# An adjacency GNN pair on one core: fewer matmuls in P, diagonals on GpSimd, setup and last group in a new order

## What is computed

```python
h = relu(layernorm(x))
z_l, z_g, v = h @ W_lang.T, h @ W_grav.T, h @ W_V.T
A_l = relu(cosine(z_l, z_l)) * not_eye          # rows of z_l normalized
A_g = exp(-|z_g_n - z_g_m|**2 / (2 sigma**2)) * not_eye
K   = w_l * rows(A_l * adj) + (1 - w_l) * rows(A_g * adj)   # rows(): divided by the row's sum
x = x + (K @ v) @ W_O.T
h = relu(layernorm(x))
x = x + (adj * adj).T @ h + bias                # per batch
```

## Time and profile before

| | |
|---|---|
| median of 3 runs | 1214.26 us |
| profiled execution | 1213.74 us, span 1212.0 us |
| TensorE busy | 1190.9 us, 98% of the span, 5968 matmuls |
| VectorE busy | 1120.8 us, 92%, 1919 instructions |
| ScalarE busy | 707.0 us, 58% |
| GpSimd busy | 609.5 us, 50%, 988 instructions |
| chain that ended last | TensorE 94%, VectorE 3%, ScalarE, DMA, issue and SPq 1% each |
| chain by line | L1040 50%, L1131 27%, L1109 15% |

### The profile page before, as it was taken

The page is one execution under the profiler, slowest core; times in us unless marked ns, Lnnn a source line. Parts: engine busy times, 40 slices in busy tenths (PEclk is TensorE's granted clock), DMA queues, the critical chain, the costliest instruction groups (busy, mean ns, idle before and its releaser), DMA issues.

```text
span 1212.0 us, 22868 instructions
## 1 busy us (share of the span) xinstructions
PE 1190.9 (98%) x5968; PEld 1009.5 (83%) x5968; DVE 1120.8 (92%) x1919; ACT 707.0 (58%) x1326; POOL 609.5 (50%) x988
## 2 busy tenths in 40 slices
PE   7999999999999999999999999999999999999996
PEld 6887888888888888888888888888888888888884
DVE  6678999999999999999999999999999999999878
ACT  5355556666556666555656555666655566655544
POOL 2103655545565555565454566554556545546543
PEclk9999999999999999999999999999999999999998
DMA  7333555554554564555565455555455556445412
GB/s 258 100 120 90 166 161 166 190 176 154 170 168 149 178 193 154 165 165 157 168 194 170 150 175 163 157 181 188 152 170 165 151 169 199 159 158 159 136 48 104
DMA packets 182416, 193.85 MB, mean 160 GB/s; under 512 B 20352, under 2 KB 131584, under 8 KB 182400
## 3 DMA queue, kind: packets, MB, share of 16 engines
q1 hardware_dynamic: 181824, 193.33, 51.2%
q10 hardware_dynamic: 576, 0.33, 0.1%
HBM read 103.09 MB, written 90.50 MB: 160 GB/s over the span
## 4 chain that ended last, share of the span: by engine, by line
PE 94%; DVE 3%; ACT 1%; DMA 1%; issue 1%; SPq 1%; POOL 0%; ACTq 0%; DVEq 0%
PE ring L1040 50%; PE ring L1131 27%; PE p_ps L1109 15%; PE ring L1158 1%; DVE x_ring L750 0%; DMA x_ring<-in_L_gnn_W_lang 0%; SPq L256 0%; DVE chain L900 0%; ACT h L481 0%; PE ring L1167 0%; DMA h<-p_dram 0%; DVE deg L716 0%; SPq L286 0%; DVE K L730 0%; DVE hT_lo L669 0%
## 5 line engine op out<-in xcount | busy, mean ns | idle before, releaser
L398 POOL TENSOR_TENSOR h_lo<-h2f,h_hi 128x512 fp32r<-128x512 f32 x124 | 157.1, 1298 | 301.7 <-ACT h_hi L584 301.6
L1040 PE MATMUL ring<-hT_hi,Lw_hi 128*128 128x512 f32 x640 | 249.4, 390 | 4.2 <-DVE hT_lo L689 1.5
L1040 PE MATMUL ring<-hT_hi,Lw_lo 128*128 128x512 f32 x640 | 249.0, 389 | 0.0
L1040 PE MATMUL ring<-hT_lo,Lw_hi 128*128 128x512 f32 x640 | 249.0, 389 | 0.0
L502 ACT ACTIVATE y_hi<-ring 128x512 fp32r<-128x512 f32 x256 | 148.5, 592 | 111.8 <-PE ring L1040 109.0
L552 ACT ACTIVATE v_hi<-ring 128x512 fp32r<-128x512 f32 x128 | 76.4, 598 | 227.5 <-PE ring L1131 158.8
L1131 PE MATMUL ring<-MT_hi,hT_hi 128*128 128x512 f32 x512 | 203.0, 397 | 0.3 <-DVE v_lo L669 0.3
L1131 PE MATMUL ring<-MT_lo,hT_hi 128*128 128x512 f32 x512 | 199.9, 390 | 0.0
L1131 PE MATMUL ring<-MT_hi,hT_lo 128*128 128x512 f32 x512 | 199.5, 390 | 0.0
L383 POOL TENSOR_TENSOR x_ring<-x_ring,bias_sb 128x512 f32 (+1 forms) x120 | 166.2, 1406 | 48.1 <-DVE KT_lo L746 48.1
L669 DVE TENSOR_TENSOR y_lo<-ring,y_hi 128x512 fp32r<-128x512 f32 x256 | 166.9, 681 | 19.6 <-ACT y_hi L502 19.6
(11 more groups left out here) (187 smaller groups left out, 2503.1 us busy)
## 6 DMA issues: line engine op xcount, KB each, us to landing
x_ring<-in_x SPq DMA_DIRECT2D x32, 1024.0 KB, 5.3
out<-x_ring SPq DMA_DIRECT2D x128, 256.0 KB, 2.5
h_dram<-h SPq DMA_DIRECT2D x62, 512.0 KB, 3.4
h_turned<-h_dram SPq DMA_DIRECT2D x248, 128.0 KB, 3.3
p_dram<-chain SPq DMA_DIRECT2D x62, 256.0 KB, 2.1
h<-p_dram SPq DMA_DIRECT2D x248, 64.0 KB, 2.6
rn_cols<-rn_dram SPq DMA_DIRECT2D x31, 256.0 KB, 3.9
k_dram<-chain SPq DMA_DIRECT2D x31, 256.0 KB, 2.0
```

The costliest lines, as they stand in the source:

```text
L398: pool.tensor_tensor(h2[1][:, b], h2f[:, b], h2[0][:, b].bitcast(F32), ALU.subtract)\
L1040: mm = pe.matmul(out, lhsT, rhs, start=(k == 0), stop=(k == len(terms) - 1))
```

## The change

- P: in the first row block (a = 0) the third pass, hT_lo·y_hi, is dropped: 8 matmuls for 4 batches and not 12. So that S still has it, y of that block takes its pass hT_lo with M0, the diagonal block that isn't halved, and not with Lw_hi; ScalarE makes two M0 copies in setup.
- `diagonal` of all groups but the last goes to GpSimd. GpSimd's order is now: wait for `k_ready`, two `add_bias`, four `h2_lo`, wait for `kt_split`, both diagonals, `row_norms`. VectorE: `kt_lo`, `squares(0)`, `v_lo(0)`, `squares(1)`, the clip.
- Setup: x(0) is loaded ahead of W_grav, which comes in four loads, and x(1) waits for the last of them; x_stats(0) stands ahead of W_grav's split; TensorE starts with 20 transposes of the identity, and transposes h(0) in the middle of W_grav's product; Lw of l = 1 is finished behind h; all of W_O is transposed inside iteration 0; group 1 is normalized after all y blocks of iteration 0.
- Last group: `shift` after v_hi(0), one of the four adds and the statistics behind the row factors, KT_hi ahead of v_hi(3), two layer 1 products ahead of K·v, the factors of group 30 in two halves, and GpSimd's h2_lo and last factors interleaved otherwise.

The core of the diff ("..." for lines left out; moves of adj_sb and adj2 into the tile chain, and bookkeeping of banks and semaphores, are left out too):

```diff
@@ -228,6 +231,17 @@
         spread = y_rows[0][:, 1, 0:P]
+        select = diag_of[:, :, :].rearrange("p l m -> p (l m)").unsqueeze(1).to_broadcast([P, GB // 2, 2 * P])
+        def diagonal(eng, g, q):
+            half = slice(q * GB // 2, (q + 1) * GB // 2)
+            if q == 0:
+                wait_for(eng, k_stored, 16 * g)
+            eng.wait_ge(p_copied, 2 * g + q + 1)
+            eng.tensor_tensor(diag[:, half].rearrange("p b l m -> p b (l m)"),
+                              P_sb[:, half].rearrange("p b l m -> p b (l m)"), select, ALU.mult)\
+               .then_inc(diag_ready, 1)
@@ -307,11 +321,14 @@
                 sp.dma_start(raw_l[:, c], w_rows[:, c]).then_inc(w_loaded[f"l{c}"], 16)
-            sp.dma_start(raw_g, w_grav.rearrange("(c p) n -> p c n", p=P)).then_inc(w_loaded["g"], 16)
             load_x(0)
+            g_rows = w_grav.rearrange("(c p) n -> p c n", p=P)
+            for c in range(C):
+                sp.dma_start(raw_g[:, c], g_rows[:, c]).then_inc(w_loaded[f"g{c}"], 16)
...
             sp.wait_ge(x_loaded, 16)
+            sp.wait_ge(w_loaded[f"g{C - 1}"], 16)
@@ -355,23 +372,24 @@
                                    base=0, pattern=[[-1, P]], channel_multiplier=1).then_inc(ident_ready, 1)
-            def std_factors(g, bn, bn_done, t, step):
-                pool.wait_ge(bn_done, GB * (g + 1))
+            def std_factors(g, bn, bn_done, t, step, b0=0, b1=GB, steps=0):
+                bn, t = bn[:, b0:b1], t[:, :, b0:b1]
+                pool.wait_ge(bn_done, GB * g + b1)
@@ -407,12 +425,18 @@
                 if lag:
+                    pool.wait_ge(k_ready, i)
+                    add_bias(i - 2, 0)
+                    add_bias(i - 2, 1)
...
                         h2_lo(i - 2, b)
-                    pool.wait_ge(kt_split, i)
-                    add_bias(i - 2, 0)
-                    add_bias(i - 2, 1)
+                if after:
+                    if before:
+                        pool.wait_ge(kt_split, i)
+                    for q in range(2):
+                        diagonal(pool, i, q)
@@ -425,7 +449,9 @@
                         .then_inc(bias_split, 1)
-                    norm2(i - 1)
+                    pool.wait_ge(h2_done, GB * (i - 1))
+                    for q in range(2):
+                        std_factors(i - 1, bn2, bn2_done, ln2, ln2_step, q * HALF, (q + 1) * HALF, LN_STEPS * q)
@@ -451,18 +477,18 @@
                     .then_inc(ln2_rstd, 1)
+            h2_lo(g - 1, 0)
             last_factors(0)
-            h2_lo(g - 1, 0)
             h2_lo(g - 1, 1)
+            h2_lo(g - 1, 2)
             last_factors(1)
-            h2_lo(g - 1, 2)
@@ -502,20 +528,23 @@
                         n += 1
-                        if not before and n <= 2:
-                            factor_hi(C + 2 * n - 2)
-                            factor_hi(C + 2 * n - 1)
+                        if not before:
+                            for q in {2: [C], 3: [C + 1], 4: [C + 2, C + 3], 5: [0, 1], 6: [2], 7: [3]}.get(n, []):
+                                factor_hi(q)
...
                             exponentials(i - 1)
-                        if after and n == 5:
+                        if before and after and n == 5:
...
                             w_g_K_g(i - 1)
-                        if after and n == 7:
+                        if before and after and n == 7:
                             normalize(i + 1, GB // 2)
+                if not before:
+                    normalize(i + 1, 0)
+                    normalize(i + 1, GB // 2)
@@ -544,6 +572,8 @@
                         exponentials(i)
+                    if not after and b == GB - 1:
+                        kt_copy(i)
@@ -554,10 +584,9 @@
                         w_g_K_g(i)
-                    if b == 1 and after:
+                    if b == (1 if after else 0):
...
                 if not after:
-                    kt_copy(i)
@@ -565,6 +594,8 @@
                     act.wait_ge(ln2_rstd, 2 * (1 + b // (GB // 2)))
+                elif isinstance(g, int) and g == NG - 2:
+                    act.wait_ge(ln2_step, LN_STEPS * (g + 1 + b // HALF))
@@ -624,6 +657,8 @@
                     act.wait_ge(setup_mm, C * l + c + 1)
+                    if c == 0:
+                        act.activation(M0[:, l], banks[c][:, 0:P], ACT.Copy)
@@ -801,8 +832,10 @@
                         if not before:
-                            for q in {1: [C], 2: [C + 1], 3: [C + 2, C + 3], 4: [0, 1], 5: [2], 6: [3]}.get(n, []):
+                            for q in {2: [C], 3: [C + 1], 4: [C + 2, C + 3], 5: [0, 1], 6: [2], 7: [3]}.get(n, []):
                                 factor_lo(q)
+                            if n == 3:
+                                x_stats(1, 0, GB)
@@ -813,9 +846,12 @@
                             turn_K(i - 1)
-                        if after and n == 6:
+                        if before and after and n == 6:
...
                             turn_blocks(i + 1, 1)
+                if not before:
+                    turn_blocks(i + 1, 0)
+                    turn_blocks(i + 1, 1)
@@ -830,12 +866,10 @@
                 if before:
-                    diagonal(i, 0)
...
                     squares(i, 0)
-                    diagonal(i, 1)
+                    v_lo(0)
                     squares(i, 1)
-                    v_lo(0)
@@ -888,21 +922,11 @@
                 dve.tensor_tensor(A, p_ps[:, :, :, :], P_sb, ALU.add).then_inc(s_ready, 2)
-            select = diag_of[:, :, :].rearrange("p l m -> p (l m)").unsqueeze(1).to_broadcast([P, GB // 2, 2 * P])
-            def diagonal(g, q):
+            def squares(g, q):
...
                     wait_for(dve, p_shifted, g)
-                    wait_for(dve, k_stored, 16 * g)
-                dve.wait_ge(p_copied, 2 * g + q + 1)
-                dve.tensor_tensor(diag[:, half].rearrange("p b l m -> p b (l m)"),
-                                  P_sb[:, half].rearrange("p b l m -> p b (l m)"), select, ALU.mult)\
-                   .then_inc(diag_ready, 1)
-            def squares(g, q):
-                half = slice(q * GB // 2, (q + 1) * GB // 2)
@@ -920,28 +943,30 @@
                     lo(v[1][:, b], bank(n + v_use(b, True)), v[0][:, b], hi + b + 1).then_inc(drained, 1)
-                diagonal(i, 0)
+                diagonal(dve, i, 0)
...
                 squares(i, 0)
-                diagonal(i, 1)
+                diagonal(dve, i, 1)
...
                 v_lo(0)
-                for b in range(GB):
+                for b in range(3):
                     add(i - 1, b, n + 1 + b)
-                dve.wait_ge(drained, use + G_USES + 1 + GB)
-                dve.wait_ge(ln2_step, LN_STEPS * (i - 1))
-                stats(i - 1, 0)
...
                 row_factors(i)
+                add(i - 1, 3, n + 1 + 3)
+                dve.wait_ge(drained, use + G_USES + 1 + 3)
+                dve.wait_ge(ln2_step, LN_STEPS * (i - 1))
+                stats(i - 1, 0)
+                combine(i)
+                stats(i - 1, 1)
                 v_lo(1)
-                combine(i)
+                kt_lo(i)
                 v_lo(2)
-                stats(i - 1, 1)
-                kt_lo(i)
                 v_lo(3)
+                dve.wait_ge(drained, use + G_USES + 1 + GB)
@@ -1043,9 +1066,13 @@
                 free(use)
-                product(bank(n), [t for c in range(a + 1) for t in passes(
+                terms = [t for c in range(a + 1) for t in passes(
                     [w[:, l, blk[a, c]] for w in Lw],
-                    [w[:, c].rearrange("p b m -> p (b m)") for w in hT])]).then_inc(g_done, 1)
+                    [w[:, c].rearrange("p b m -> p (b m)") for w in hT])]
+                if a == 0:
+                    terms[1] = (M0[:, l], terms[1][1])
+                product(bank(n), terms).then_inc(g_done, 1)
@@ -1090,11 +1117,13 @@
                     for l in range(2):
+                        if not before and l == 1:
+                            pe.wait_ge(side_split, a + 1)
...
                         n += 1
-                        if not before and n == 2:
-                            transposes_w_o(C // 2)
-                            transposes_w_o(C // 2 + 1)
+                        if not before and 2 <= n <= 3:
+                            transposes_w_o(2 * n - 4)
+                            transposes_w_o(2 * n - 3)
@@ -1104,6 +1133,7 @@
                         terms = passes([w[:, a, b] for w in hT], [w[:, a, b].rearrange("p l m -> p (l m)") for w in y])
+                        terms = terms[:2] if a == 0 else terms
@@ -1151,6 +1181,10 @@
                 return passes([w[:, e, c * P:(c + 1) * P] for w in parts], [w[:, e, c * P:D] for w in parts])
+            pe.wait_ge(ident_ready, 1)
+            for _ in range(WARM):
+                pe.transpose(bank(C - 1)[:, 0:P], ident[:, :], ident[:, :])
@@ -1160,6 +1194,10 @@
             for c in range(C):
+                if c == C // 2:
```

(20 more changed lines are left out.)

60 lines of the change are left out of this document (28 added, 32 removed).

## The result

The changed kernel takes 1218.71 us (median of 8 runs, 1216.85 to 1219.85), the kernel before 1214.35 us on the same chip (8 runs): ratio 1.0034, 95% interval 1.0024 to 1.0044. It is slower by 0.3%, where 1197.5 us, 1.4% faster, was forecast. The profiled execution has a span of 1217.4 us against 1212.0.

The account below looks back on a forecast made before the run. TensorE bounds the kernel at 35.88 us a group; afterwards the loop through all queues does, at 35.59. From 1213.7 us, P(31) ending 11.9 earlier and the last group's 4.3 leave 1197.5 us, range 1189.5 to 1209.

Parts of the forecast that it names:

- Rival A: Group loop: TensorE stays the bound, at a period of 35.4 us with no gaps; 1191.8 us, chance 0.20.
- rival C: GpSimd's diagonals: each costs 1.57 us and not 1.27, the loop becomes 36.2 us; 1214 us, chance 0.07.
- The place of TensorE's wait: Group loop: TensorE's K·v or V(1) held by KT_lo or v_lo, some 0.2 us a group.
- The loop after the change: From one first add to the next through rn_cols and K: five terms sum to 35.59 us, 35.76 before.
- the term from k_ready to the first add: KT_lo 8.3, two diagonals 2.54, squares 1 0.69, clip 0.16 less 0.1, hand-overs 0.15: 11.74 us, before 11.91.
- GpSimd's queue, plus 0.55: KT_lo can't finish before GpSimd's six operations end, k_ready + 7.7, plus about 0.55: 8.3 us.
- the issue of rn_cols: Loop term from the end of turn_p(1) to the issue of rn_cols: 2.31 us.
- the three other terms: First add to the end of turn_p(1) 8.29 us, rn_cols' landing 3.9, landing to k_ready 9.35.
- the 1.06 us of diagonal 0: VectorE's diagonal before the change, set against GpSimd's 1.27; the trace was said not to show a factor of 2.
- Rival D: K's return: K lands 7.6 us after k_ready, not 6.9, KT_lo ends at 9.0, loop 36.3; 1217 us, chance 0.10.
- Setup and first groups: y(0) at 24.4 us, net 2.4 earlier, bounds 1 and 4; first add of iteration 1 2.8 earlier.
- The last group: After P(31): reordered chain gains 4.3 us, bounds 2 (GpSimd's factors, unhidden) and 6 (none of these delays).

Follow-up runs that it names:

- e4: Changed kernel with P's two turned halves made earlier on VectorE and ScalarE's shift of P moved earlier: 1209.92 us, ratio 0.9958 to the kernel before.
- e9: Changed kernel with diagonal 0 ahead of KT_lo, diagonal 1 behind it, then h2_lo(2) and (3); squares(1) and clip ahead of v_lo(0): 1197.39 us, ratio 0.9862.
- e12: Changed kernel with the setup of the kernel before (W_grav ahead of x(0), no 20 first transposes): 1216.79 us, ratio 1.0028 to the kernel before.
- e3: Changed kernel with the diagonals back on VectorE and GpSimd's and VectorE's orders as before: 1207.93 us, ratio 0.9942 to the kernel before.

## Why the prediction was wrong, point by point

**The mechanism was right in the main.** The loop takes over from TensorE, the diagonals cost 1.29 us on GpSimd against 1.27 forecast, GpSimd is through its queue 0.55 us before KT_lo ends and waits for it, the landings of K and rn_cols average 6.87 and 3.88 against 6.9 and 3.9. Rival A (TensorE stays the bound) and rival C (1.57 a diagonal) are refuted. The place of TensorE's wait was wrong: it is y(0), behind the last hT_lo, and not K·v or V(1). The forecast followed the loop through rn_cols alone; that the late first add also delays hT_lo it left out, and e4 shows that this second path holds the period at 35.95 once the first is shortened.

**The step that failed is the sum of "The loop after the change", in it the term from k_ready to the first add**: the loop took 36.26 and not 35.59 us, 28 times 0.67 = 18.8 us of the 21.6 by which the profiled execution missed. That is also why the sign was wrong: 35.59 is under the 35.88 of before, 36.26 is over it. By its terms:
- k_ready to first add, 11.74 forecast, 12.31 measured. KT_lo ends at 8.48 and not 8.3: the rule "GpSimd's queue, plus 0.55" held, but 7.7 was six durations without the 0.33 us until GpSimd starts. From KT_lo to the first diagonal it is 0.25 us, and from diagonal 1 to the first add 1.04 and not 0.90: I had 0.15 us for all hand-overs together. A hand-over from VectorE to GpSimd costs 0.25 to 0.33 us by these rows, and the edit adds two to the path.
- the issue of rn_cols, 2.31 forecast, 2.43 measured: the late DMA in four of the 26 groups.
- the three other terms held to 0.03 us.

That GpSimd holds KT_lo back, and so both diagonals behind it, was in the forecast but taken as given; e9 shows that another order of the same work is worth 21 us, nearly all of it through diagonal 0 ahead of KT_lo and not through KT_lo itself, which ends only 0.09 us earlier there.

**A price read wrongly.** The forecast took the 1.06 us of diagonal 0 as VectorE's own price. But it was held too: h2_lo runs until 557.64, and diagonal 0 ends at 558.19, 0.55 us behind it. Alone the same diagonal takes 0.67 us, as the last group below shows. So the factor of about 2 that the forecast didn't find in the trace is there: 1.27 against 0.67. It changes no term of the sum, since the loop after the change has the diagonals on GpSimd.

**Rival D** had nearly the right time (1217) and the right threshold, a loop over 36.2 us, for a wrong reason: K does not land at k_ready + 7.6 in the steady groups.

**The range.** Each 0.1 us in the loop is 2.8 us in the end. The sum was 0.19 over TensorE, and of its terms only the landings and C's price were given bounds; the hand-overs, five of them at 0.04 to 0.33 us, had none. With 0 and 0.3 us as their ends the range would have reached above 1215, and the sign would have been open.

**Setup and first groups.** y(0) starts at 25.22, 2.2 us earlier, and 24.4 was forecast; P(1) ends 2.3 earlier, forecast 3.3. GpSimd in the setup of the changed kernel shows part of it, four of norm1's ten steps:

```profile
14.15 0.57 POOL L379 TENSOR_TENSOR ln<-bn 128x4 f32<-128x4 f32 x1 [11.37 <-DVE bn L711]
14.68 0.65 POOL L380 TENSOR_TENSOR ln<-bn 128x4 f32<-128x4 f32 x1
15.29 0.65 POOL L381 TENSOR_TENSOR ln<-bn 128x4 f32<-128x4 f32 x1
...
16.62 0.20 POOL L384 TENSOR_SCALAR ln<-ln 128x4 f32<-128x4 f32 x1
```

While VectorE splits W_grav (13.99 to 16.48, operations with two SBUF inputs) a step of 4 columns takes 0.65 us, afterwards 0.20. That is 1.6 us in front of the normalization, which h's transposes and the rest of W_grav's product wait for, and the change put these two side by side. The first transposes did what was counted: W_lang's 48 matmuls then take 8.0 us, as forecast, where the earlier trace rows had 9.85. What the setup gave is gone at the end: with W_grav in four DMAs, rn_cols is issued 3.0 us late in four groups together, and against e12 the changed kernel is 1.0 us ahead at k_ready(1) and 2.2 behind at k_ready(29).

**The last group.** From P(31)'s end to the span's end 42.6 us, before 44.9: 2.3 gained, 4.3 forecast, within the bounds of 2 to 6. It starts late: at P's end GpSimd is still in h2_lo, which costs VectorE 1.9 us:

```profile
1174.95 1.48 DVE L241 TENSOR_TENSOR chain<-chain,diag_of 128x512 f32<-128x512 f32 x1 [3.55 <-ACT chain L559]
1176.36 1.78 DVE L777 TENSOR_TENSOR KT_lo<-K,KT_hi 128x512 fp32r<-128x512 f32 x1
1178.06 0.67 DVE L931 TENSOR_REDUCE sq<-chain 128x4 f32<-128x512 f32 x1
1178.66 0.67 DVE L241 TENSOR_TENSOR chain<-chain,diag_of 128x512 f32<-128x512 f32 x1
...
1198.59 1.27 DVE L795 SCALAR_TENSOR_TENSOR ln<-ln 128x2 f32<-128x2 f32 x1
```

The same diagonal takes 0.67 us alone and 1.48 beside h2_lo. sum_s_last starts at P's end + 7.75 (forecast 7.2), KT is split at + 18.4 (17.4), the first output starts at + 25.1 (24.5), the output of (30, 3) at + 31.9 (30.3). From KT's split to the end VectorE is the chain, with adds, statistics and outputs, and not TensorE.

## What to carry to other kernels

An operation moved to another engine is priced by its place in that engine's queue, not by its duration: here, against the diagonals on VectorE (e3), the same 1.29 us diagonals cost 11 us when both stand behind KT_lo and win 10 when one stands before it and one behind, with VectorE's order to match. When a sum comes within a few tenths of a microsecond of a second bound in a loop of 30 turns, every hand-over between engines (0.25 to 0.33 us from VectorE to GpSimd) needs a term and a bound of its own. After an early operation is won, look at what stands behind it in the next engine's order (squares(1) behind v_lo(0)), or the gain stops there.

## What the runs showed of the hardware that was not expected

- GpSimd and VectorE keep each other out for whole instructions whatever their size: a GpSimd step of 128x4 goes from 0.20 to 0.65 us, a VectorE step of 128x2 from 0.16 to 1.27, KT_lo from 0.69 to 1.54 and 1.78. A VectorE operation of 128x512 ends about 0.55 us behind the GpSimd one that blocked it. VectorE's adds that read one input from PSUM are not held (0.68 us beside h2_lo in e9). The Trainium skill (SBUF — State Buffer, section "SBUF: two separate sides") has the lock, for a VectorE operation with two SBUF inputs, and these rows agree with it. The clip has one SBUF input and is held all the same, 0.52 us for 0.17 beside h2_lo in e9; no run asked why.
- The norms' store lands 0.6 to 2.0 us late in groups 4, 9, 14 and 19 of every kernel, 160 DMAs apart, but not in group 24. With W_grav in four DMAs and not in one, P(0)'s store just before it lands 0.5 to 1.7 us late in these groups too, and in the changed kernel that costs 0.4 to 1.1 us each at the issue of rn_cols. What is behind it is open: a fixed count of DMAs isn't, since the norms' store is late both as it stands and with three more DMAs ahead of it.
